# Narrow attention: a group's four indirect row transfers, issued one per beat behind residual sums

## The reference

```python
qh = (q @ Wq + bq).reshape(B, LQ, 16, 8)...      # narrow cross attention
attn = softmax(qh @ kh.T * scale); out = attn @ vh @ Wo + bo
x = layernorm(x + out)
expert = argmax(x @ centroids.T)                 # per token, 8 experts
x = layernorm(x + alpha * y[expert] + (1 - alpha) * x)
```

## Time and profile before

| | |
|---|---|
| median of 3 runs | 3711.24 us (3711.16 to 3727.55) |
| span of the profiled execution | 3714.9 us |
| TensorE busy | 3331.5 us, 90% |
| mean granted TensorE clock | 0.940 |
| this phase, from its first load to its last transfer | about 2940 to 3490 us |
| indirect transfers in the phase | 64, median 962 ns each on GpSimd |

### The profile page before, as it was taken

How to read it: one execution, slowest core, us unless ns; L and a number is a source line. 1 busy time by engine, 2 the same in 40 slices (tenths; PEclk the granted TensorE clock), 3 DMA queues, 4 the chain that set the end, 5 groups by cost and what they waited for, 6 DMA issues and landing times. The chain is left out here.

```text
span 3714.9 us, 102284 instructions
## 1 busy us (share of the span) xinstructions
PE 3331.5 (90%) x41297; PEld 2126.3 (57%) x41297; DVE 2389.2 (64%) x5654; ACT 1972.6 (53%) x3558; POOL 2002.1 (54%) x1774
## 2 busy tenths in 40 slices
PE   7999999996999999879999999969999799999586
PEld 3554555543555555655666667735555466666475
DVE  5888888885455555675666648667777544444365
ACT  5666666653566665434565544346666354444254
POOL 4777887774777787661111126337777412212265
PEclk8999999998999999998999999979999788888698
DMA  4222222225700000000000000000000000000264
GB/s 145 88 83 85 85 85 90 89 83 167 223 2 2 2 2 2 15 10 6 5 5 5 3 6 1 8 7 2 2 2 2 12 20 22 14 11 10 72 179 118
DMA packets 50282, 164.67 MB, mean 44 GB/s; under 512 B 11823, under 2 KB 23218, under 8 KB 40785
## 3 DMA queue, kind: packets, MB, share of 16 engines
q1 hardware_dynamic: 45520, 150.43, 12.6%
q0 software_dynamic: 4352, 8.47, 0.7%
HBM read 149.89 MB, written 43.65 MB: 52 GB/s over the span
## 5 line engine op out<-in xcount | busy, mean ns | idle before, releaser
L496 DVE TENSOR_TENSOR_SCAN XC<-ssm_dA,ssm_db 128x2048 f32<-128x2048 f32 x128 | 565.5, 4418 | 109.3 <-PE ssm_db L352 96.4
L559 POOL TENSOR_TENSOR XC<-XC,XB 128x1536 f32<-128x1536 f32 x128 | 505.8, 3952 | 179.7 <-DVE XC L496 136.0
L366 PE MATMUL ssm_y<-XC,weights 128*128 128x512 f32 x1024 | 472.5, 604 | 2.5 <-POOL XC L559 2.3
L445 ACT ACTIVATE ssm_dA<-ssm_delta,ssm_nega 128x508 f32<-128x508 f32 x512 | 325.1, 707 | 84.1 <-DVE XC L496 83.5
L1173 POOL TENSOR_TENSOR self_pm<-self_pT,weights 128x512 f32<-128x512 f32 x256 | 322.2, 1302 | 64.8 <-ACT self_pT L911 64.2
L366 PEld LDWEIGHTS ssm_y<-XC,weights 128*128 128x128 f32 x1024 | 187.6, 190 | 215.8 <-issue 204.4
L1179 POOL TENSOR_TENSOR XC<-XC,XB 128x128 f32<-128x128 f32 x128 | 60.0, 470 | 399.3 <-DVE XB L1058 399.3
L1599 DVE TENSOR_REDUCE narrow_nmax<-narrow_scores 128x4 f32<-128x308 f32 x256 | 106.4, 472 | 207.7 <-PE narrow_scores L1372 138.4
L2571 POOL TENSOR_TENSOR XC<-XC,weights 128x512 f32<-128x512 f32 x128 | 161.8, 1285 | 111.0 <-ACT XC L2407 111.0
L1044 DVE TENSOR_REDUCE self_nmax<-self_scores 128x4 f32<-128x512 f32 x256 | 158.5, 682 | 88.6 <-PE self_scores L794 88.6
L352 PEld LDWEIGHTS ssm_db<-XB,ssm_dxT 32*128 32x128 f32 x4096 | 135.0, 188 | 99.3 <-DVE XC L496 65.0
(11 more groups left out here) (429 smaller groups left out, 8308.6 us busy)
## 6 DMA issues: line engine op xcount, KB each, us to landing
XB<-c_rows SPq DMA_DIRECT2D x64, 1024.0 KB
sorted<-in_padding SPq DMA_DIRECT2D x1, 33280.0 KB, 114.6
experts_we<-in_w_experts SPq DMA_DIRECT2D x72, 323.0 KB, 3.1
experts_rt<-sorted SPq DMA_DIRECT2D x72, 65.0 KB
ssm_xT<-in_xT SPq DMA_DIRECT2D x16, 256.0 KB
XC<-in_w_experts SPq DMA_DIRECT2D x9, 256.0 KB
weights<-in_w_self SPq DMA_DIRECT2D x1, 1412.0 KB, 7.5
cross_ctx_t<-in_ctx SPq DMA_DIRECT2D x16, 77.0 KB
```

Source lines behind the costliest of these rows:

```text
L366: mm = pe.matmul(yp[half][:, :].rearrange("p (b t) -> p b t", b=GROUP), ident, of_state(states(32, at), k), start=(k == 0 and nq == 0 and ...
L445: o = act.activation(dA[:, p % 2, :].rearrange("p (b k t) -> p b k t", b=GROUP, k=4)[:, :, k, 1:T], by_batch(delta[:, slot, half, :])[:, : ...
L496: dve.tensor_tensor_scan(states(0, p).rearrange("p m t -> p (m t)"), dA[:, p % 2, :], db[:, :], 0.0, ALU.mult, ALU.add).then_inc(h_ready, 1)
L559: pool.tensor_tensor(states(32, p).rearrange("p (b k) t -> p b k t", k=4)[:, :, 0:3, :], states(0, p).rearrange("p (b k) t -> p b k t", k= ...
```

## The change

One wait is put ahead of each of the four transfers of a group. Transfer b of group g waits until `out_read`, the count of residual sums done, is at least 4g + 10 + b, and at most 64.

```diff
                 pool.wait_ge(pick_step, PICK * g + 1)
                 pool.wait_ge(place, PLACE * (g + 1))
                 for b in range(GROUP):
+                    pool.wait_ge(out_read, min(g * GROUP + 10 + b, N))
                     at = pos[:, g * GROUP + b:g * GROUP + b + 1]
                     pool.indirect_dma_start(table, bass.IndirectOffsetOnAxis(ap=at, axis=0),
                                             row[:, g % RING * GROUP + b, :], None).then_inc(scattered[g % RING], 16)
```

## The result

| | kernel before | changed kernel |
|---|---|---|
| median of 4 runs beside each other | 3719.39 us | 3678.19 us |
| profiled execution, its span | 3714.9 us | 3654.8 us |
| mean granted TensorE clock in it | 0.940 | 0.953 |
| this phase, from its first `scaled` to its last | 477.3 us | 426.3 us |

The account below looks back on a forecast made before the run. TensorE was taken to bound the phase. Per group, -2.0 us of stall and +1.25 of clock gave -0.75, times 13 = -10 us, hence 3701 us (chance 0.34); own range 3688 to 3717, all cases 3655 to 3768.

Parts of the forecast that it names:

- clock holds: Phase beats: with a stall of 1.5 us in place of 3.78 the clock never falls; 47 us won, 3664; chance 0.22.
- What bounds the phase: TensorE bounds the phase; a group's transfers go with 5.07 us, over 13 groups, so 66 us is all to win.
- Where the waits put the transfers: Transfers 0 and 1 still go back to back; only 2 goes one beat later and 3 two beats later.
- What is queued behind them costs nothing: GpSimd's `residual` and `inv` queued behind the waits: covered by idle of 18 us each, so no cost.
- The pair, 1.5 us: Beat of transfers 0 and 1: matmuls lose 1.06 us, late maxima 1.70; a stall of 1.5 was taken.
- T0: Start of a group's first transfer, at 3405.65 in the timeline before; the forecast's stall times count from it.
- A transfer alone, 0.15 us each: Beats of transfers 2 and 3: effect ends at 1.99 us, matmuls never pause; 0.15 us taken for each.
- The clock: TensorE's clock still falls to 1.2 GHz once a group, now nearly all over work; costs 1.25 us more than before.
- price of low clock over work: Each us at 1.2 GHz where TensorE works costs 0.43 us; 6.6 us of it cost 2.85 a group.
- A quarter each: Each transfer costs its quarter of the stall in any beat: 3740 with lower clock, chance 0.22; 3690 with clock up, 0.06.
- lone ones dearer: Transfers 2 and 3, alone, cost more than in a train: 7.24 us in place of 3.78, 3772 us; chance 0.12.
- not the transfers: Something else in the long beat stops TensorE, so the time stays 3711 us; chance 0.04.

Follow-up runs that it names:

- mixed kernels: Two kernels sending each group's rows differently (none, alone, pairs, three, four in train, plain transfers), against the kernel before: 3680.67 us beside 3697.74, and 3678.56 beside 3727.12.

## Why the prediction was right, and where it failed

**The number.** The direction was right and 3678 us lies in the range over all cases, but that range (3655 to 3768) holds nearly all the rivals. It does not lie in the forecast's own range, 3688 to 3717, but between the forecast and the rival "clock holds" (3664). In the terms of the sum, a group's stall was to shrink by 2.0 us and shrank by 2.33 (10.25 less 7.92); the clock was to take back 1.25 and instead gave 1.2 more in the profiled execution (3.5 less 2.33). That the range held is owed to the rivals in it, not to the forecast's mechanism.

**What bounds the phase.** Right where the stall exists: groups without transfers take 25.87 us, and TensorE is busy all through. That the long beat comes from the transfers is shown by the mixed kernels, within one trace. Not foreseen: on two of the chips the same program with the same transfers has no stall, and there the change is worth nothing (1.0015).

**Where the waits put the transfers.** Right: 0 and 1 in train, 2 and 3 alone behind a sum.

**What is queued behind them costs nothing.** Right as far as the traces show: on the chip without a stall the phase took 409.6 us with the waits and 410.9 without. The ratio of the runs there, at most 1.0025, would leave room for 9 us.

**The pair, 1.5 us.** 7.92 or 7.93 less 6.47 is 1.46. Right. The working behind it holds in its course: the pause of matmuls was shorter (0.31 us where 1.06 had been worked out, partly because by the earlier trace rows the first pause begins at T0 + 2.49 and not at 2.2), and the late maxima (T0 + 3.00; 3.26 had been worked out) decided.

**A transfer alone, 0.15 us each.** Right, and nearly 0: the four together cost 0.03 us. The reason given, that 2.2 us pass before matmuls pause, holds only half: a lone transfer does delay TensorE's signals, for some 1.4 us from its start, and the maxima are needed just after that.

**The clock.** The step that failed: "Up to T0 + 3 the new kernel does what the old one does, so the clock still falls there". In the profiled execution the clock stayed at 1.00 through all four beats of 10 of the 13 groups, and 3.5 us were saved in each such group (30.8 less 27.3): x 13 = 46, where the rival "clock holds" had worked out 47, and 3664 us in all. The premise holds: up to T0 + 3 both beats have one pause in `weighted`, of 0.31 and 0.33 us. What doesn't follow from it is the fall. In the trace before, the clock fell between T0 + 2.9 and T0 + 4.9 in the 13 groups (T0 + 3.09 in rows 5); in the changed kernel's it fell in one pair's beat, at T0 + 2.95. The difference that the rows show is what comes after: the pair's beat runs full, the old one goes on pausing. Why the clock held in groups where TensorE had done the same up to T0 + 3 isn't shown. But that rival isn't the whole truth either. Whether the clock falls behind a pair differs from group to group and from execution to execution (1 and 6 groups of 13), and the medians, 3678 and 3684, lie between the two cases. The forecast's price of low clock over work (0.43 us for each us) was right.

The rule of the Trainium skill that the prediction weighed (its page TensorE: Matmul & The Clock Gate, section "HAM oscillation — how this bites in real kernels") would have let each lone transfer bring a low stretch of its own. The traces don't bear that out: in one execution with all transfers alone only two low stretches of 6.8 us were left in the phase, in the other five and a longer one at its end, and the kernel without transfers, on a chip without the stall, had five. The page speaks of waits in which TensorE stands idle; a lone transfer leaves it none (6.53 us busy of 6.53), so its case isn't this one.

**The other rivals.** A quarter each, lone ones dearer, and not the transfers: all three fall by the windows of the mixed kernel.

## What to carry to other kernels

Where a stall belongs to a train of transfers, look in the new profile whether any still stand in train: the change left one pair in each group, and starting transfers 1 to 3 one beat later still was worth another 35 us. And time the kernel before again beside every set of runs: two sets without the stall would have said that the change does nothing.

## What the runs showed of the hardware

The same program takes about 3641 to 3646 us in some sets of runs and 3698 to 3727 in others, at equal transfers, and the difference lies in these beats: 6.50 us or 10 us. Between the two traces of the kernel before, this phase makes 66.4 of the 71.6 us (477.3 and 410.9). Two sets of runs with the same chip number, less than half an hour apart, showed one 3645.85 and the other 3727.12; whether it was the same chip in two conditions or two chips isn't recorded. What makes the difference stays open.

Where the stall exists, TensorE's signals are late beside indirect transfers of GpSimd (ScalarE starts 0.9 us later beside a single one, 2.05 us after `sums` in place of 1.15), and they aren't beside plain ones from GpSimd or SyncE with the same rows. The Trainium skill, in SBUF — State Buffer, section "Who interferes with whom", has TensorE and ScalarE wait for nobody. That section is on the ports of SBUF, and no run here says whether a port has a part in this; but the trace has both wait: ScalarE's step starts later beside an indirect transfer, and TensorE pauses beside four. That it is the signals that are held back, and that TensorE stops when too many are outstanding, is a reading of the timelines and wasn't tested by itself.

The next phase issues four indirect transfers in train as well, and isn't longer where the stall exists (from the last `scaled` to the end 251.9 us, and 252.8 without it); which signals would have to be late there wasn't looked into.
